# Attention scores from two rounded 32-bit parts, two heads at once on the two halves of TensorE's rows

## The chip, the core and the metric

One core of a Trainium2 chip runs the whole program. The metric is the device time of one execution in microseconds (us), the median of several runs. A core has five engines that are programmed apart and meet by semaphores: TensorE (PE; its weight loads have rows of their own, PEld), VectorE (DVE), ScalarE (ACT), GpSimd (POOL) and SyncE (SP), which only issues transfers here. A queue name with a q (SPq, ACTq) stands for the transfers that the engine issues.

## What is computed

A "macaron" block on 16 sequences of 512 tokens and 256 features: half a feed-forward step with 16 routed and 2 shared experts, then attention with 16 heads of 16 features, then half a feed-forward step again. Cut to what matters:

```python
def attn(x, Wq, bq, Wk, bk, Wv, bv, Wf, bf):          # x: (16, 512, 256), already layer-normed
    q, k, v = heads(x @ Wq + bq), heads(x @ Wk + bk), heads(x @ Wv + bv)
    # heads 0..7 look back only, heads 8..15 look ahead only, with a slope on the distance
    fwd = slopes * tril(rel) + triu(-1e9, 1)
    bwd = slopes * triu(-rel) + tril(-1e9, -1)
    scores = einsum('bhqd,bhkd->bhqk', q, k) / sqrt(16) + concatenate([fwd, bwd])
    out = einsum('bhqk,bhkd->bhqd', softmax(scores), v)
    return out.transpose(0, 2, 1, 3).reshape(B, S, D) @ Wf + bf

x = x + 0.5 * ffn(layernorm(x))
x = x + attn(layernorm(x))
x = x + 0.5 * ffn(layernorm(x))
```

## The kernel before

**Stages.** The feed-forward step works in groups of sequences: layer norm, routing, the two shared experts, then the routed tokens are scattered to memory sorted by expert, read back as tiles of 256 rows ("tile transpose" L1071, "tile hidden" L1081, "tile out" L1092), written and gathered again. Attention runs sequence by sequence (b = 0 to 15) in four groups of four heads (g = 0 to 3). Feed-forward tiles of both layers are woven in between, so that all engines serve both.

**One group of heads.** Scores are computed twice. First with queries on the rows ("row", L1132), only to get each query's largest score: ten units u of up to 512 columns for the four heads, each in one bank of PSUM. A unit of the first four is one product of 512 columns; one of the next four is a product of 384 and one of 128 columns; the last two have two of 256. A further product adds -1e9 beyond the diagonal: the identity times a mask of -1e9 (L1148). DVE takes the maxima (L1566, L1559). Their negatives are split into two parts (L1657, L1660), turned by a small transposition on PE (L1154), copied by ACT (L1346) and sent by a transfer into two further rows of the query stack (L1349). Then the scores are computed with keys on the rows ("score", L1165), now with the maximum already subtracted by those two rows, again in ten units. ACT takes the exponential of each (L1325), POOL zeroes what lies beyond the diagonal (L1782), and PE multiplies by the values (L1185, four heads side by side on 32 columns of the array each).

**The stacks.** `q_stack` and `k_stack` hold, for each head, the numbers that one product contracts: six blocks of 16 rows that pair three bfloat16 parts of q with three of k (QB, KB), three rows for the slope, and two for the maximum: 99 or 101 rows. ACT (L1302), DVE (L1643), ACT (L1307) and POOL (L1769) split q and k into the three parts, and SP scatters them in 6 transfers for q and 6 for k for each half m of the heads (L922). The stacks exist once: the half m = 0 (groups 0 and 1) of the next sequence can be scattered only after the last score of group 1, the half m = 1 after that of group 3. PE waits for the last of the 12 transfers before the first "row" of the half.

**What sets the order.** `schedule()` plays the program through with a list of due times and costs and writes one order for each engine; it also hands out PSUM's eight banks (`BANKS`: at most three at a time for "row", two for "score", one for the outputs, three for the feed-forward work). Each engine then runs its list strictly in order.

**Shape of PE's work.** A product whose contraction has at most 64 rows and starts at row 0 or 64 uses one half of the array's rows: "tile out" does so for its two halves (L1092). A product with 32 output columns uses a quarter of the columns (L1185, L1154). All others use the whole array. Below, a change from one of these three shapes to another in PE's order is called a change of shape.

## Time and profile before

| | |
|---|---|
| median of 3 runs | 2115.41 us (2111.2 to 2123.95) |
| the profiled execution, its own time | 2112.85 us, of which the span is 2111.1 us |
| PE busy | 1678.2 us (79% of the span) |
| DVE busy | 1477.3 us (70%) |
| ACT busy | 1041.3 us (49%) |
| POOL busy | 946.5 us (45%) |
| first "row" to last "score" | 384 to 1901 us |

How to read it: a busy time is the union of an engine's instructions. A matmul's duration holds the time in which its results drain, which overlaps the next matmul. What a matmul costs is therefore read from the step between two starts. Attention fills 384 to 1901 us; the stretch before is the first feed-forward group, the one behind is the last.

### The profile page before, as it was taken

Reading aid. Unit: us, or ns where it says so; the run is one execution under the profiler, and the core shown is the slowest. Engines: PE = TensorE matmul, PEld = TensorE weight load, DVE = VectorE, ACT = ScalarE, POOL = GpSimd, SP = SyncE. Lnnn points to the kernel's source line nnn. Section 1 sums busy time; section 2 is a strip of 40 time slices with the busy share of each in tenths; the row PEclk is TensorE's granted clock in tenths of the full one; section 3 lists DMA queues with packets and bytes.
Section 4 is the critical chain, followed back from the end, with each engine's and each line's share of the span. In section 5 each row is a group of like instructions: output and inputs, shape, how many; then the busy total and the mean of one; then the engine's idle time right before and its main releaser. Section 6 shows DMA issues by size and latency. Waiting matters only on the chain. (4 is left out here: it accounts for less than half of the span.)

```text
span 2111.1 us, 35275 instructions
## 1 busy us (share of the span) xinstructions
PE 1678.2 (79%) x10696; PEld 1106.3 (52%) x10696; DVE 1477.3 (70%) x3920; ACT 1041.3 (49%) x2263; POOL 946.5 (45%) x999
## 2 busy tenths in 40 slices
PE   2769885778898898889887988889887777897571
PEld 2656664546565564555454655656554444565440
DVE  4886666779866675787968778677786875765352
ACT  3335543355555655555544565556554344554241
POOL 1653337554524231546534444253545656131544
PEclk8889996899999998998988999999998779899786
DMA  7368862747878777565648776586647686865995
GB/s 211 137 217 291 257 201 93 143 97 202 231 181 237 190 222 168 157 102 123 134 100 232 191 182 184 147 202 143 172 96 145 208 236 169 207 205 177 322 362 171
DMA packets 327978, 392.79 MB, mean 186 GB/s; under 512 B 40296, under 2 KB 269032, under 8 KB 327784
## 3 DMA queue, kind: packets, MB, share of 16 engines
q1 hardware_dynamic: 260816, 267.81, 49.1%
q0 software_dynamic: 24576, 67.14, 11.1%
q10 hardware_dynamic: 42400, 55.59, 8.4%
q8 instruction: 88, 1.44, 0.3%
q14 instruction: 98, 0.80, 0.1%
HBM read 188.58 MB, written 155.19 MB: 163 GB/s over the span
## 5 line engine op out<-in xcount | busy, mean ns | idle before, releaser
L1325 ACT ACTIVATE p_buf<-bank 128x512 f32<-128x512 f32 x640 | 358.4, 598 | 228.1 <-PE bank L1165 193.0
L1566 DVE TENSOR_REDUCE row_max<-bank 128x1 f32<-128x512 f32 (+2 forms) x768 | 348.4, 502 | 119.8 <-PE bank L1148 117.6
L1782 POOL TENSOR_SCALAR_AFFINE_SELECT p_buf<-p_buf 128x512 f32<-128x512 f32 x256 | 160.4, 641 | 387.2 <-ACT p_buf L1325 386.2
L1132 PE MATMUL bank<-k_stack,q_stack 99*128 99x512 bf16 (+3 forms) x1024 | 249.9, 319 | 37.0 <-issue 29.8
L1165 PE MATMUL bank<-q_stack,k_stack 101*128 101x512 bf16 (+3 forms) x1024 | 239.3, 318 | 50.1 <-DMA q_stack<-shift_t 37.1
L1725 POOL DMA_INDIRECT sorted_x<-xn,position x224 | 221.2, 988 | 91.7 <-issue 52.1
L1748 POOL DMA_INDIRECT y_tok<-sorted_y,position x192 | 185.4, 966 | 130.2 <-DVE x_att L1637 52.1
L1185 PE MATMUL bank<-p_buf,v_rows 128*32 128x512 f32 (+3 forms) x2048 | 188.1, 468 | 37.5 <-POOL p_buf L1782 36.7
L1291 ACT ACTIVATE t_y<-bank 128x256 f32<-128x256 f32 x406 | 133.3, 381 | 128.3 <-PE bank L1092 106.3
L1081 PE MATMUL bank<-t_xt,t_w 128*128 128x256 f32 x548 | 157.0, 413 | 34.8 <-DMA t_w<-expert_w 25.8
L1619 DVE SCALAR_TENSOR_TENSOR t_g<-t_th,bank 64x256 f32<-64x256 f32 x203 | 82.5, 407 | 136.3 <-ACT t_th L1282 134.6
L1148 PE MATMUL bank<-cbf 128*128 128x256 bf16 (+1 forms) x640 | 169.4, 265 | 0.0
L1165 PEld LDWEIGHTS bank<-q_stack,k_stack 101*128 101x128 bf16 x1024 | 85.0, 101 | 153.3 <-issue 52.2
L1132 PEld LDWEIGHTS bank<-k_stack,q_stack 99*128 99x128 bf16 x1024 | 95.0, 103 | 130.9 <-issue 70.6
L1276 ACT ACTIVATE t_xt<-bank 128x512 f32<-128x512 f32 x203 | 118.9, 595 | 71.3 <-PE bank L1071 62.7
L1282 ACT ACTIVATE t_th<-bank 64x256 f32<-64x256 f32 x203 | 76.2, 375 | 131.1 <-PE bank L1081 106.8
L1081 PEld LDWEIGHTS bank<-t_xt,t_w 128*128 128x128 f32 x548 | 101.7, 202 | 67.4 <-DMA t_w<-expert_w 31.3
L1755 POOL TENSOR_TENSOR hs_buf<-h_buf,hs_buf 128x512 fp32r<-128x512 f32 x64 | 81.8, 1278 | 119.9 <-ACT hs_buf L1246 119.2
L1667 DVE RECIPROCAL den<-den 128x128 f32<-128x128 f32 x128 | 109.2, 910 | 30.5 <-DMA den<-o_store 30.3
L1624 DVE TENSOR_TENSOR t_h<-bank,t_g 64x128 f32<-64x128 f32 x406 | 119.2, 294 | 13.3
L974 PE MATMUL bank<-w_down,hs_buf 128*128 128x256 f32 x256 | 82.5, 322 | 52.1 <-POOL hs_buf L1755 50.4
L1092 PE MATMUL bank<-t_w,t_h 64*128 64x256 f32 x548 | 100.5, 444 | 17.0 <-DVE t_h L1624 15.6
(193 smaller groups left out, 3807.6 us busy)
## 6 DMA issues: line engine op xcount, KB each, us to landing
t_w<-expert_w SPq DMA_DIRECT2D x137, 256.0 KB
t_x<-sorted_x SPq DMA_DIRECT2D x137, 256.0 KB, 4.2
sorted_y<-t_y SPq DMA_DIRECT2D x137, 256.0 KB
q_stack<-qk_part SPq DMA_DIRECT2D x192, 128.0 KB
k_stack<-qk_part SPq DMA_DIRECT2D x192, 128.0 KB, 6.8
sorted_x<-zeros SPq DMA_DIRECT2D x69, 256.0 KB, 3.6
p_buf<-expert_w SPq DMA_DIRECT2D x66, 256.0 KB, 4.8
p_buf<-sorted_x SPq DMA_DIRECT2D x66, 256.0 KB, 4.7
```

Of the source, the lines that this page charges most:

```text
L1081: ins = pe.matmul(ps[:, 0:RT], weights[:, P * d:P * d + P], xt[:, d, :], start=(d == 0), stop=(d == ND - 1))
L1132: pe.matmul(ps[:, col:col + k1 - k0], q_stack[0:ROWS_S, h, P * qt:P * qt + P], k_stack[0:ROWS_S, h, k0:k1], start=(n == 0), stop=False, sk ...
L1148: ins = pe.matmul(dst, ident_bf, mask, start=False, stop=True, skip_group_check=True)
L1165: ins = pe.matmul(ps[:, col:col + q1 - q0], k_stack[0:ROWS_P, h, P * kt:P * kt + P], q_stack[0:ROWS_P, h, q0:q1], start=(n == 0), stop=Tru ...
L1185: ins = pe.matmul(ps[VR * hh:VR * hh + VR, q0:q1], v_rows[b % 2][:, v0:v0 + VR], p_of(u)[:, col:col + q1 - q0], start=(r == 0), stop=(r == 2),
L1291: act.activation(t_y[i][:, t, :], psum("ty", *of, t)[:, 0:D], ACT.Copy).then_inc(*ty_out.step(*of, t))
L1325: act.activation(p_of(u), psum("score", *of)[:, :], ACT.Exp).then_inc(*exp_done.step(*of))
L1566: ins = dve.tensor_reduce(row_max[g % 2][:, n:n + 1], src[:, col:col + q1 - q0], X, ALU.max)
L1624: dve.tensor_tensor(t_h[i][ME * t:ME * t + ME, :], ps[ME:P, at], t_g[:, at], ALU.mult).then_inc(*th_step.step(*of, "u", t))
L1725: pool.indirect_dma_start(sorted_x[l, group_of(l, b)], bass.IndirectOffsetOnAxis(ap=position[:, b, k, t:t + 1], axis=0), xn[buffer][:, t, ...
L1748: pool.indirect_dma_start(y[:, k, t, :], None, sorted_y[l, g], bass.IndirectOffsetOnAxis(ap=position[:, b, k, t:t + 1], axis=0)).then_inc( ...
L1782: pool.affine_select(blocks, blocks, [[0, GH], [1 if ahead else -1, P]], ALU.is_ge, zero, base=0, channel_multiplier=-1 if ahead else 1).t ...
```

## The change

The split is now into two parts that keep 32-bit storage (fp32r, the rounded form that the matmul reads), so three blocks of 16 rows pair them, with two rows for the slope and two for the maximum: 50 or 52 rows. Two heads share a stack slot, one on rows 0 to 51, one on rows 64 to 115. A pair of units of two such heads (`rows`, `scores`) is issued in turn, one on each half of the array, into two banks, and signalled once. The mask product contracts 64 rows in place of 128, one on each half; its two factors give sums of terms up to -2^30 beyond the diagonal. The third part's steps on ACT and POOL are gone. The scatter still has 6 transfers for q and 6 for k of 128 KB each, now 64 rows of 2 KB; the maxima go in two transfers instead of one, one for each half. `BANKS` allows four banks for "row" and four for "score".

```diff
-ROWS_S = 6 * HD + 3
+QB = (0, 0, 1)
+KB = (0, 1, 0)
+ROWS_Q = len(QB) * HD
+ROWS_S = ROWS_Q + 2
 ROWS_P = ROWS_S + 2
-QB = (0, 0, 0, 1, 1, 2)
-KB = (0, 1, 2, 0, 1, 0)
...
-BANKS = {"row": 3, "score": 2, "out": 1, "fill": 3, "wide": 6}
+BANKS = {"row": 4, "score": 4, "out": 1, "fill": 3, "wide": 6}
...
-                part(at + 0.38 * u, "PE", 0.33 if u < 4 else 0.4, piece, *stacks, takes=takes, lag=0.3)
+                part(at + 0.76 * v, "PE", 0.45 if v < 2 else 0.5, rows, *stacks, takes=takes, lag=0.3)
...
-                part(t + at + 0.6 + 0.1 * w, "ACT", 0.62, rest, (qk, "DVE"))
-                part(t + at + 0.6 + 0.1 * w, "POOL", 1.17, rest, (rest, "ACT"))
...
-        q_stack = sb("q_stack", [P, H, S], BF16)
-        k_stack = sb("k_stack", [P, H, S], BF16)
+        q_stack = sb("q_stack", [P, SLOTS, S], F32R)
+        k_stack = sb("k_stack", [P, SLOTS, S], F32R)
...
-                    sp.wait_ge(*qk_third.at(*of))
+                    sp.wait_ge(*qk_step.at(*of))
                     stack, parts = ((q_stack, QB), (k_stack, KB))[n]
-                    for blk in range(6):
-                        sp.dma_start(stack[HD * blk:HD * blk + HD, HB * m:HB * m + HB, :],
-                                     qk_part[n][:, parts[blk], :]).then_inc(*scattered[n, m].step(b, blk))
+                    for blk in range(3):
+                        for half in range(2):
+                            low = HALF * half
+                            sp.dma_start(stack[low + HD * blk:low + HD * blk + HD, SLOTS // 2 * m:SLOTS // 2 * (m + 1), :]
+                                         .bitcast(F32), qk_part[n][low:low + HALF, parts[blk], :].bitcast(F32)
+                                         ).then_inc(*scattered[n, m].step(b, blk, half))
...
+                    both_u = 2 * v, 2 * v + 1
+                    two = [take(("row", b, g, u), max_done, b, g, u) for u in both_u]
+                    for n in range(len(unit_tiles(g, 2 * v))):
+                        for ps, u in zip(two, both_u):
+                            hh, r = unit_tiles(g, u)[n]
+                            (low, slot), qt, col = place_of(g, hh), row_tile(g, hh, r), row_col(g, hh, r)
+                            k0, k1 = keys(GH * g + hh, qt)
+                            at = slice(low, low + ROWS_S)
+                            pe.matmul(ps[:, col:col + k1 - k0], q_stack[at, slot, P * qt:P * qt + P],
+                                      k_stack[at, slot, k0:k1], start=(n == 0), stop=False, skip_group_check=True)
...
+                    for ps, low in zip(two, (0, HALF)):
+                        at = slice(low, low + HALF)
+                        mask = right[at, :]
...
+                        ins = pe.matmul(dst, left[at, :], mask, start=False, stop=True, skip_group_check=True)
...
-                    act.dma_start(q_stack[ROWS_S:ROWS_P, GH * p:GH * p + GH, :], shift_t[p % 2][:, :]
-                                  ).then_inc(*shift_row[p % 2].step(b, p))
+                    for half in range(2):
+                        low = HALF * half
+                        act.dma_start(q_stack[low + ROWS_S:low + ROWS_P, 2 * p:2 * p + 2, :].bitcast(F32),
+                                      shift_t[p % 2][GH * NT * half:GH * NT * half + GH * NT, :]
+                                      ).then_inc(*shift_row[p % 2].step(b, p, half))
```

PE's order, at the first "row" units of sequence 8, group 1. In the kernel before, L1165 is a score, L1132 a row product and L1148 its mask; the bank written stands ahead of the arrow.

```order
L1165 MATMUL bank2<-q_stack,k_stack 128x384
L1165 MATMUL bank2<-q_stack,k_stack 128x128
L1132 MATMUL bank5<-k_stack,q_stack 128x512
L1148 MATMUL bank5<-cbf 128x128
L1165 MATMUL bank7<-q_stack,k_stack 128x384
L1165 MATMUL bank7<-q_stack,k_stack 128x128
L1132 MATMUL bank6<-k_stack,q_stack 128x512
L1148 MATMUL bank6<-cbf 128x128
L1165 MATMUL bank0<-q_stack,k_stack 128x384
L1165 MATMUL bank0<-q_stack,k_stack 128x128
L1185 MATMUL bank4<-p_buf0,v_rows1 32x512 x4
```

The same place in the changed kernel, where L1197 is a score, L1160 a row product, L1176 its mask and L1217 the values.

```order
L1197 MATMUL bank7<-q_stack,k_stack 128x384
L1197 MATMUL bank1<-q_stack,k_stack 128x384
L1197 MATMUL bank7<-q_stack,k_stack 128x128
L1197 MATMUL bank1<-q_stack,k_stack 128x128
L1160 MATMUL bank6<-k_stack,q_stack 128x512
L1160 MATMUL bank2<-k_stack,q_stack 128x512
L1176 MATMUL bank6<-cbf 128x128
L1176 MATMUL bank2<-cbf 128x128
L1217 MATMUL bank5<-p_buf0,v_rows1 32x512 x4
```

Each product now stands beside its twin in another bank, and the two kinds of score work are next to each other in the half-array shape. Counted over PE's whole order, the changes of shape are 804 before and 1096 in the changed kernel. Before, a step into the whole-array shape begins with a bfloat16 product (mostly L1132, L1165) 224 times and with a 32-bit one 152 times; a step into the half-array shape begins with a 32-bit one 201 times; 227 steps go into the quarter-column shape. In the changed kernel these are 8, 398, 470 and 220.

ACT's order around the maxima's transfer of one group, in the kernel before: L1325 is an exponential, L1346 and L1349 the copy and the transfer of the maxima, L1332 and L1335 the output.

```order
L1325 ACTIVATE p_buf1<-bank2 128x512
L1325 ACTIVATE p_buf1<-bank7 128x512
L1325 ACTIVATE p_buf1<-bank0 128x512
L1325 ACTIVATE p_buf1<-bank3 128x512
L1346 ACTIVATE shift_t0<-bank2 32x128
L1349 DMA q_stack<-shift_t0 2x16x128
L1325 ACTIVATE p_buf2<-bank1 128x512
L1325 ACTIVATE p_buf2<-bank0 128x512
L1332 ACTIVATE o_raw<-bank4 128x512
L1335 DMA o_store<-o_raw 128x512
```

The same group in the changed kernel (L1353 is an exponential, L1374 and L1379 the maxima's copy and transfers, L1360 and L1363 the output).

```order
L1353 ACTIVATE p_buf1<-bank2 128x512
L1353 ACTIVATE p_buf1<-bank4 128x512
L1353 ACTIVATE p_buf1<-bank7 128x512
L1353 ACTIVATE p_buf1<-bank1 128x512
L1353 ACTIVATE p_buf2<-bank4 128x512
L1353 ACTIVATE p_buf2<-bank3 128x512
L1374 ACTIVATE shift_t0<-bank1 32x128
L1379 DMA q_stack<-shift_t0 2x8x128 x2
L1360 ACTIVATE o_raw<-bank5 128x512
L1363 DMA o_store<-o_raw 128x512
```

Here the maxima's copy stands two exponentials later against the group that is being finished, and it issues two transfers.

## Rows read from the trace of the kernel before

**Rows 1.** The page: busy us of each engine, share of the span, instructions.
```profile
PE 1678.2 (79%) x10696; PEld 1106.3 (52%) x10696; DVE 1477.3 (70%) x3920; ACT 1041.3 (49%) x2263; POOL 946.5 (45%) x999
```
**Rows 2.** Windows: length; busy us (count) PE, PEld, DVE, ACT, POOL; clock; DMA; GB/s.
```profile
384.00:1901.00 1517.00, 1290.65 (x8624) 815.47 (x8625) 1135.65 (x2843) 812.76 (x1731) 675.92 (x731) 0.93 0.69 173
1541.00:1555.00 14.00, 10.07 (x75) 6.69 (x75) 10.28 (x31) 7.58 (x17) 1.28 (x3) 1.00 0.89 137
1700.00:1800.00 100.00, 80.30 (x493) 49.56 (x493) 65.23 (x160) 46.88 (x99) 55.51 (x59) 0.86 0.75 205
```
**Rows 3.** Waits from 384 to 1901 us: who for whom, total us, times, longest.
```profile
PE bank L1165 <- DMA q_stack<-shift_t: 37.1, 15, 6.2
PE bank L1185 <- POOL p_buf L1782: 36.7, 40, 4.2
DVE row_max L1566 <- PE bank L1148: 117.6, 65, 9.9
ACT p_buf L1325 <- PE bank L1165: 193.0, 127, 13.0
SPq L922 <- PE bank L1165: 122.5, 23, 18.8
```
**Rows 4.** Timeline of PE: start us, us, line, operation, count; bfloat16 units.
```profile
1227.17 0.38 PE L1132 MATMUL bank<-k_stack,q_stack 99*128 99x512 bf16 x1
1227.39 0.22 PE L1148 MATMUL bank<-cbf 128*128 128x128 bf16 x1
1227.44 0.38 PE L1132 MATMUL bank<-k_stack,q_stack 99*128 99x512 bf16 x1
...
1231.26 0.39 PE L1132 MATMUL bank<-k_stack,q_stack 99*128 99x384 bf16 x2
...
1231.60 0.38 PE L1132 MATMUL bank<-k_stack,q_stack 99*128 99x384 bf16 x2
```
**Rows 5.** Timeline of PE: rounded 32-bit products of 512 and 256 columns.
```profile
1211.44 0.40 PE L975 MATMUL bank<-act_t,w_attn 128*128 128x512 f32 x1
1211.68 0.40 PE L976 MATMUL bank<-act_t,w_attn 128*128 128x512 f32 x1
1212.00 0.70 PE L1092 MATMUL bank<-t_w,t_h 64*128 64x256 f32 x4
1212.64 0.39 PE L1132 MATMUL bank<-k_stack,q_stack 99*128 99x512 bf16 x1
...
1203.41 0.28 PE L975 MATMUL bank<-w_down,hs_buf 128*128 128x256 f32 x1
1203.52 0.28 PE L976 MATMUL bank<-w_down,hs_buf 128*128 128x256 f32 x1
```
**Rows 6.** Timeline of PE: full 32-bit products, and a small one of another shape.
```profile
1216.11 1.03 PE L1081 MATMUL bank<-t_xt,t_w 128*128 128x256 f32 x4
1216.97 0.60 PE L1165 MATMUL bank<-q_stack,k_stack 101*128 101x512 bf16 x3
...
1244.75 0.23 PE L1154 MATMUL bank<-cbf,shift 128*32 128x128 bf16 x1
1244.91 0.39 PE L1165 MATMUL bank<-q_stack,k_stack 101*128 101x384 bf16 x2
```
**Rows 7.** Page, costliest groups: weight loads of bfloat16 and of 32 bits, mean ns.
```profile
L1165 PEld LDWEIGHTS bank<-q_stack,k_stack 101*128 101x128 bf16 x1024 | 85.0, 101 | 153.3 <-issue 52.2
L1081 PEld LDWEIGHTS bank<-t_xt,t_w 128*128 128x128 f32 x548 | 101.7, 202 | 67.4 <-DMA t_w<-expert_w 31.3
```
**Rows 8.** One line each: count, ns min/median/max, first and last start.
```profile
L1307 ACT ACTIVATE qk_part<-rest x64: 616/630/652, 365.6 to 1798.5; 128x512 bf16<-128x512 f32 x64
L1769 POOL TENSOR_TENSOR qk_part<-rest,qk_part x64: 1146/1162/1413, 366.3 to 1799.2; 128x512 bf16<-128x512 f32 x64
L1349 ACTq DMA_DIRECT2D q_stack<-shift_t x64: 623/683/1274, 396.1 to 1889.7; - x64
```
**Rows 9.** Timeline of SP, the six transfers of q for one half.
```profile
1540.65 4.39 SPq L922 DMA_DIRECT2D q_stack<-qk_part  x6
```

More of the change, by code:

```diff
@@ L40 @@
 RT = 256
-N_BIAS = 6
+N_BIAS = 10
 N_ONES = 3
@@ L393, in gathering @@
         tail = y_buffer(l, b) > 0
-        needs = [(("score", B - 1, NG - 1, UNITS - 1), "PE")] if tail else []
+        needs = [(("scores", B - 1, NG - 1, PAIRS - 1), "PE")] if tail else []
         if (l, b) == (0, 0):
@@ L464, in schedule @@
             stacks = [(("qk put", b, g // 2, w), "SP") for w in range(2)]
[L465 to L468 removed]
+            for v in range(PAIRS):
+                rows, two = ("rows", b, g, v), [("row", b, g, u) for u in (2 * v, 2 * v + 1)]
+                takes = [bank("row", piece, (piece, "DVE")) for piece in two]
+                if v == 0:
                     takes.append(("pair", ("pair", b, g), [(("shift out", b, g), "ACT landed")]))
[L470 to L471 removed]
+                part(at + 0.76 * v, "PE", 0.45 if v < 2 else 0.5, rows, *stacks, takes=takes, lag=0.3)
+                for piece in two:
+                    part(at + 0.76 * v, "DVE", 0.83 if v in (2, 3) else 0.69, piece, (rows, "PE"))
             shift, out = ("shift", b, g), ("shift out", b, g)
@@ L476, in schedule @@
             part(at + 3.9, "ACT", 1.1, out, (out, "PE"), lag=3.4)
-            for u in range(UNITS):
-                score, c = ("score", b, g, u), set_of(u)
-                s = at + 4.9 + 0.38 * u
-                part(s, "PE", 0.3, score, (out, "ACT"), takes=[bank("score", score, (score, "ACT"))], lag=0.3)
-                takes = [(f"p{c}", ("p", b, g, c), [(("values", b, g, c), "PE")])] if u == SETS[c][0] else []
-                part(s, "ACT", 0.6, score, (score, "PE"), takes=takes)
+            for v in range(PAIRS):
+                scores, two = ("scores", b, g, v), [("score", b, g, u) for u in (2 * v, 2 * v + 1)]
+                s = at + 4.9 + 0.76 * v
+                part(s, "PE", 0.4, scores, (out, "ACT"),
+                     takes=[bank("score", score, (score, "ACT")) for score in two], lag=0.3)
+                for score in two:
+                    u, c = score[3], set_of(score[3])
+                    takes = [(f"p{c}", ("p", b, g, c), [(("values", b, g, c), "PE")])] if u == SETS[c][0] else []
+                    part(s, "ACT", 0.6, score, (scores, "PE"), takes=takes)
             for c, (u0, u1) in enumerate(SETS):
@@ L515, in schedule @@
                 part(t + at + 0.3 * w, "DVE", 0.75, qk, (qk, "ACT"))
-                part(t + at + 0.6 + 0.1 * w, "ACT", 0.62, rest, (qk, "DVE"))
-                part(t + at + 0.6 + 0.1 * w, "POOL", 1.17, rest, (rest, "ACT"))
-                used = [(("score", b - 1, 2 * m + 1, UNITS - 1), "PE")] if b else [(("stack rows",), "SP")]
-                part(t + (12.7, 20.7)[m], "SP", 3.6, put, (rest, "POOL"), *used, lag=6.0)
+                used = [(("scores", b - 1, 2 * m + 1, PAIRS - 1), "PE")] if b else [(("stack rows",), "SP")]
+                part(t + (12.7, 20.7)[m], "SP", 3.6, put, (qk, "DVE"), *used, lag=6.0)
         for half in range(2):
```

246 lines of the change are left out of this document (120 added, 126 removed).

## The prediction

> **What bounds the kernel now.** I read the page first: PE is the busiest engine with 1678 us, DVE has 1477, ACT 1041 [rows 1]. Then the windows: attention runs from 384 to 1901 us, and there PE is busy for 1291 of 1517 us (85%), DVE for 1136 (75%), ACT for 813, at a mean granted clock of 0.93 [rows 2]. Then the waits of that stretch: ACT waits for a score product 193 us in all, DVE for a masked row product 118 us, while PE waits for ACT or DVE seldom; its longest totals are the transfer of the maxima, 37 us, and POOL's mask, 37 us [rows 3]. So the evacuating engines wait for PE more than PE for them, and no engine is full: PE's order is the nearest thing to a bound, with latencies in its gaps. A second loop runs beside it. SP waits 122 us for the last score before it may scatter the next half [rows 3], then the first six transfers alone take 4.4 us to issue [rows 9], and the transfer engines are 0.89 busy in such a stretch with PE still working [rows 2]. Two halves alternate, so most of that is covered.
>
> **PE's products.** A unit of the row product steps by 1227.44 - 1227.17 = 0.27 us with a 128-column mask and by 1231.60 - 1231.26 = 0.34 us with a 256-column one [rows 4]. 0.22 of either is the 512 columns, which is also a score unit. One group: 4 x 0.27 + 6 x 0.34 + 10 x 0.22 = 5.3 us, and 64 groups 340 us.
>
> After, 512 columns of fp32r step by 0.24 us and 256 by 0.115 [rows 5]. Do two half-array products overlap? L1092 is such a pair, in full 32 bits: four records, and the next instruction starts 0.64 us later [rows 5]. Two products of the same width one after the other on the whole array, L1081, take 0.86 us [rows 6]. Half of 0.86 is 0.43, so the pair overlaps fully and 0.21 us is something else (below). Per pair of units I take the price of one: 512 columns and mask 0.24 + 0.05; 384 and 128 with a 256-column mask 0.18 + 0.06 + 0.11; twice 256 with its mask 0.23 + 0.11. Rows of one group: 2 x 0.29 + 2 x 0.35 + 0.34 = 1.6 us. Scores: 2 x 0.24 + 2 x (0.18 + 0.11) + 0.23 = 1.3 us, where the 128-column piece is given the 0.11 us of a weight load that nothing longer covers. 64 x 2.9 = 186 us. **Saved: 340 - 186 = 154 us.**
>
> No fp32r product of 128 columns is in the trace, and each group has 4 pairs of them. Bounds: 0.06 us (by column) and 0.215 us (the rate of full 32 bits, half of L1092's 0.43). At the upper end 4 x about 0.13 us x 64 = 32 us of the saving are gone. I take the lower, since 256 and 512 columns of this type step by column; both ends go into the range.
>
> **PE's changes of shape.** The small transposition L1154 has 128 columns, 0.05 us by column, and the next product starts 0.16 us later [rows 6]: the change itself costs 0.10 us. After L1092 and L976 the two changes and one uncovered 32-bit weight load come to (0.32 - 0.24) + 0.21 = 0.3 us [rows 5]. So a change into a bfloat16 product, or to 32 output columns, costs 0.10 to 0.11 us, and one into a 32-bit product with 128 output columns 0.20, since its load comes on top. That fits the loads' records, 101 ns for bfloat16 and 202 for 32 bits [rows 7]. By the counts under the change: before 224 x 0.10 + 353 x 0.20 + 227 x 0.11 = 118 us, after 8 x 0.10 + 868 x 0.20 + 220 x 0.11 = 199 us. **Lost: 81 us**, half the saving. PE's net relief is 154 - 81 = 73 us (41 with slow 128-column pieces).
>
> The Trainium skill, "TensorEngine Tiling (Array Packing)", Key Properties, says that changing the tiling mode drains TensorE; by that rule the trace agrees, at 0.10 us each. Its page "TensorE: Matmul & The Clock Gate", Weight-path perf modes, has the fast weight load only for types other than fp32; the two load durations agree. By rule and by row alike the relief is 73 us, where a count of products alone gives 154.
>
> **From PE to the end.** All of this lies between 384 and 1901 us. At clock 0.93 the 73 us are 78 us of time. PE is busy 85% there, and the transfer, maxima and mask latencies stay; DVE would stand near 79%. I let three quarters pass: 0.75 x 78 = 58 us.
>
> **The rest.** ACT loses 64 x 0.63 us of the third part and gains a second maxima transfer to issue, 64 x 0.68 us [rows 8]: +3 us, nothing. But the second transfer starts 0.68 us after the first, PE waits for both, and in ACT's order the exponentials of the next group stand behind it. PE's 15 waits for that transfer [rows 3] grow by 15 x 0.7 = 10 us. POOL loses 64 x 1.16 = 74 us [rows 8]; POOL is busy 45%, its values' masks make PE wait 37 us over 40 times, and I credit 4 us. The chain that is removed (ACT, POOL) ended before the scatter, which waits for the scores instead, so its length earns nothing; where that cover is gone it would be 1.8 us once for each half. The scatter has the same 12 transfers and the same bytes: zero. More instructions that split the attention weights, under 2 us. Sum: -58 + 10 - 4 = -52 us.
>
> The profiled execution has 2112.85 us of its own; that gives 2061. The median of the runs lies 2.6 us above it, so **2064 us**.
>
> **The rivals.**
> - *More passes than PE's relief* (0.18). The four banks for scores let PE run two pairs ahead; ACT's 193 us and DVE's 118 us of waits shrink, and both halves' loops with them. If all 78 us pass and a sixth of the 311 us of waits besides, the time is 2115 - 78 - 52 + 6 = 1991. Against it: eight banks now carry claims of 12, and the feed-forward work shares them.
> - *Slow 128-column pieces* (0.17). Relief 41 us, 44 at the clock, 33 passing, + 6: 2115 - 27 = 2088.
> - *Evacuation sets the pace* (0.13). DVE's maxima and ACT's exponentials are unchanged in number and size, and the scatter's loop is not shorter. If these bound the stretch, PE's relief becomes idle time: 2115 + 6 = 2121, at most 1% from before. For it: DVE 75% busy and in order. Against: DVE waits 118 us for PE. The Trainium skill, "TensorEngine Tiling (Array Packing)", PSUM Bottleneck, warns that tiling speeds TensorE and not the evacuation; no row here shows that it binds.
> - *The clock gives it back* (0.14), the other side. A stretch in which PE is busy 80% has a granted clock of 0.86 where the whole has 0.93 [rows 2]. PE's 1291 us minus 78 in the same 1517 would be 80%. If the clock goes to 0.86 by that, what is left, 1213 us, becomes 1213 x 0.93 / 0.86 = 1312 us, 99 more than without, against 78 saved: 21 slower, and with the 10 us of the maxima and banks that starve the feed-forward tiles, 2115 + 31 = 2146. It decides from a clock of 0.93 x 1213 / 1291 = 0.87 down. Against it: the two levels, 1.2 and 2.4 GHz, mix in every stretch, and 0.86 also came with feed-forward work that waited for transfers.
> - *The change does not do what it says*: the twins do not overlap with this type and width. Then rows and scores cost 2 x 186 = 372 us against 340, plus 81: over 100 us slower, 2230. The pair L1092 speaks against it (0.03, counted as slower).
>
> **How the numbers follow.** The forecast itself (-52, 2064, own range 2035 to 2092) has 0.35. Each way by about 1%, 21 us, is what a measurement of this kernel can tell from no change. Faster by over 1%, below 2094: forecast 0.34, more passes 0.18, most of the slow pieces 0.12, sum 0.64. Slower, above 2137: the clock 0.13 and no overlap 0.03, 0.16. Within: 0.20. The range 2000 to 2130 leaves out half of "more passes" (0.06 to 0.09) and nearly all of the slower ones.
>
> **What would show it.** In the changed profile: L1160 and L1197 in pairs with steps of 0.24 us a pair (right) or 0.48 (no overlap); the 384 and 128-column pair with its mask 0.35 us (0.50 if slow); PE's busy time in attention down by some 70 us while its instructions are fewer; granted clock still 0.92 or more; DVE near 79% there; the wait of L1197 for the maxima's transfer up by some 10 us. The prediction is wrong if the granted clock falls below 0.88, if a change of shape costs more than 0.10 us between 32-bit products, or if PE starts to wait for row_max and p_buf (the evacuation).

## The result, and the profile after

The changed kernel takes 2090.8 us (median; 2088.1 to 2095.6) against 2119.5 us of the kernel before on the same chip: a ratio of 0.987, 95% interval 0.983 to 0.991. That is 1.3% faster, some 27 us, where 52 us (2064) were forecast. It lies inside the range, and on the right side, but half of the size is missing. The profiled execution has a span of 2086.3 us (before 2111.1). Ratios here and below are taken over executions in the kernel's faster state alone, on the same chip, and can differ a little from the quotient of two medians.

The page of the changed kernel, busy us of each engine, share of the span and instructions:
```profile
PE 1646.8 (79%) x10696; PEld 1114.7 (53%) x10696; DVE 1467.1 (70%) x3924; ACT 999.8 (48%) x2205; POOL 874.8 (42%) x935
```
Against [rows 1], PE lost 31 us of busy time, POOL 72, ACT 42, DVE 10. The windows (length; busy us and count of PE, PEld, DVE, ACT, POOL; granted clock; DMA share; GB/s) of the parts ahead of, in and behind attention:
```profile
0.00:386.00 386.00, 271.00 (x1494) 214.20 (x1494) 251.20 (x814) 158.62 (x364) 181.41 (x179) 0.88 0.65 200
386.00:1874.00 1488.00, 1257.11 (x8612) 821.66 (x8612) 1123.33 (x2845) 771.13 (x1664) 608.08 (x670) 0.89 0.69 176
1874.00:2086.00 212.00, 118.69 (x593) 78.85 (x592) 92.61 (x266) 70.01 (x178) 85.34 (x87) 0.79 0.78 261
```
Attention took 1517 us before [rows 2] and takes 1488 now; the parts around it (384 and 210 us, now 386 and 212) did not move. The granted clock fell from 0.93 to 0.89. The waits from 386 to 1874 us (who for whom, total us, times, longest), to be laid beside [rows 3]:
```profile
PE bank L1197 <- DMA q_stack<-shift_t: 54.0, 23, 7.4
PE bank L1217 <- POOL p_buf L1802: 18.8, 22, 2.2
PE bank L1160 <- DVE row_max L1595: 13.9, 20, 1.8
DVE row_max L1595 <- PE bank L1176: 87.5, 63, 6.5
ACT p_buf L1353 <- PE bank L1197: 149.1, 101, 7.0
```
ACT waits for scores 149 us instead of 193, DVE for masked rows 88 instead of 118, PE for POOL's mask 19 instead of 37, and PE for the transfer of the maxima 54 instead of 37.

The timeline of PE (start us, length us, line, operation, shape, merged count) at full clock, four places:
```profile
453.24 0.73 PE L1197 MATMUL bank<-q_stack,k_stack 52*128 52x512 f32 x4
453.91 0.66 PE L1023 MATMUL bank<-c,xn 128*128 128x128 f32 x4
...
1203.43 0.50 PE L1160 MATMUL bank<-k_stack,q_stack 50*128 50x384 f32 x4
1203.77 0.28 PE L1176 MATMUL bank<-cbf 64*128 64x256 bf16 x2
1203.81 0.48 PE L1197 MATMUL bank<-q_stack,k_stack 52*128 52x512 f32 x2
1204.13 0.40 PE L1160 MATMUL bank<-k_stack,q_stack 50*128 50x384 f32 x4
1204.37 0.28 PE L1176 MATMUL bank<-cbf 64*128 64x256 bf16 x2
...
1220.12 0.51 PE L1160 MATMUL bank<-k_stack,q_stack 50*128 50x384 f32 x4
1220.46 0.29 PE L1176 MATMUL bank<-cbf 64*128 64x256 bf16 x2
1220.50 0.48 PE L1160 MATMUL bank<-k_stack,q_stack 50*128 50x384 f32 x4
...
1284.84 0.50 PE L1197 MATMUL bank<-q_stack,k_stack 52*128 52x256 f32 x4
1285.18 0.39 PE L1160 MATMUL bank<-k_stack,q_stack 50*128 50x512 f32 x2
```
Four records (384 and 128 columns on either half) step by 1203.77 - 1203.43 = 0.34 us with their first load uncovered and by 0.24 us with it covered (1204.13 to 1204.37). Two score products of 512 columns step by 0.32 us behind a mask. A whole pair of units with its mask takes 0.38 us (1220.12 to 1220.50), where two units took 2 x 0.34 in [rows 4]. Two pairs of 512 columns and the change behind them take 453.91 - 453.24 = 0.67 us, and two 256-column products on either half take 1285.18 - 1284.84 = 0.34 us. The two halves do run side by side; the twins' records start 3 ns apart. These places are typical. Over the whole trace, at full clock, where PE did not wait and the next product is a half-array one too, a pair of score units takes 0.34 us whatever its columns (medians 0.337, 0.340 and 0.342 us of 36, 12 and 22 pairs), and a pair of row units with its mask 0.384 us (medians 0.384, 0.384 and 0.387 us of 21, 47 and 22). The 0.236 us that the columns of a 512 pair would allow stands at 3 of the 36.

### The profile page after: what moved, and what is told of

The parts are those of the page before. It is cut to its first block and busy times, and to the rows that moved or that the text cites. A ratio compares the mean times of both kernels' runs of the same rounds, so it can differ in the third digit from the quotient of the medians.

```text
span 2086.3 us, 35743 instructions
## 1 busy us (share of the span) xinstructions
PE 1646.8 (79%) x10696; PEld 1114.7 (53%) x10696; DVE 1467.1 (70%) x3924; ACT 999.8 (48%) x2205; POOL 874.8 (42%) x935
## 5 line engine op out<-in xcount | busy, mean ns | idle before, releaser
L1353 ACT ACTIVATE p_buf<-bank 128x512 f32<-128x512 f32 x640 | 345.8, 601 | 199.3 <-PE bank L1197 149.1
L1197 PE MATMUL bank<-q_stack,k_stack 52*128 52x512 f32 (+3 forms) x1024 | 172.8, 408 | 78.0 <-DMA q_stack<-shift_t 54.0
L1217 PE MATMUL bank<-p_buf,v_rows 128*32 128x512 f32 (+3 forms) x2048 | 202.9, 499 | 20.5 <-POOL p_buf L1802 18.8
L1160 PE MATMUL bank<-k_stack,q_stack 50*128 50x512 f32 (+3 forms) x1024 | 171.0, 399 | 57.5 <-issue 20.9
L1106 PE MATMUL bank<-t_xt,t_w 128*128 128x256 f32 x548 | 164.7, 429 | 19.2 <-DMA t_w<-expert_w 12.8
L1197 PEld LDWEIGHTS bank<-q_stack,k_stack 52*128 52x128 f32 x1024 | 95.5, 214 | 155.8 <-DMA q_stack<-shift_t 62.8
L1160 PEld LDWEIGHTS bank<-k_stack,q_stack 50*128 50x128 f32 x1024 | 96.7, 207 | 120.9 <-issue 83.9
L1742 POOL TENSOR_TENSOR rstd_ffn<-var_eps_ffn,minus_half 128x4 f32<-128x4 f32 x32 | 33.6, 1050 | 181.0 <-DVE var_eps_ffn L1446 165.4
```

Source lines behind the costliest of these rows:

```text
L1106: ins = pe.matmul(ps[:, 0:RT], weights[:, P * d:P * d + P], xt[:, d, :], start=(d == 0), stop=(d == ND - 1))
L1160: pe.matmul(ps[:, col:col + k1 - k0], q_stack[at, slot, P * qt:P * qt + P], k_stack[at, slot, k0:k1], start=(n == 0), stop=False, skip_gro ...
L1197: ins = pe.matmul(ps[:, col:col + q1 - q0], k_stack[at, slot, P * kt:P * kt + P], q_stack[at, slot, q0:q1], start=(n == 0), stop=True, ski ...
L1217: ins = pe.matmul(ps[VR * hh:VR * hh + VR, q0:q1], v_rows[b % 2][:, v0:v0 + VR], p_of(u)[:, col:col + q1 - q0], start=(r == 0), stop=(r == 2),
L1353: act.activation(p_of(u), psum("score", *of)[:, :], ACT.Exp).then_inc(*exp_done.step(*of))
```

## Experiments: is PE's relief worth its time?

My theory after the result: the speed of PE's products is not what sets the pace, and what PE is relieved of turns into idle time and lower clock. The rival is the forecast's step, three quarters of the relief pass to the end. Where a ratio is given in this and the next sections, it is to the kernel before on the same chip; 1% is 21 us. The first four of these kernels keep the planner's order of the kernel that they start from, since nothing that the planner reads is touched (the traces of the first and of the kernel before agree in all 10056 products that both have); the fifth doesn't.

The recorded expectations use letters of their own. In this section theory A is that half-array products keep the granted clock low, theory B that a relief of PE which other latencies fill up lowers the clock, and theory E, in the run with four banks, the theory above.

**The kernel before without its mask products** (L1148 is left out, and L1132 ends the unit):
```diff
-                    ins = pe.matmul(dst, ident_bf, mask, start=False, stop=True, skip_group_check=True)
```


> The kernel before without its mask products (so the maxima are taken over masked columns too); nothing else is moved. A pure relief of PE: 4 x 0.05 + 6 x 0.11 = 0.88 us a group, 56 us in all, with no half-array product and no change of shape added. Theory A (half-array products keep the granted clock low): the clock in attention stays at 0.92 to 0.93 and the time falls by 40 to 50 us, ratio to before 0.976 to 0.981. Theory B (any relief of PE that other latencies fill up lowers the clock): clock 0.89 to 0.91, time down by 15 to 30 us, ratio 0.986 to 0.993.

Measured: 2104.6 us, ratio 0.998 (0.995 to 1.002). PE has 56 us less to do at full clock, and at most 0.5%, 11 us, of it arrives. Neither A nor B forecast that: B had the clock right (0.90) and the time not. Its window of attention and its two waits for PE, from 384 to 1901 us:
```profile
384.00:1901.00 1517.00, 1264.06 (x7985) 775.32 (x7986) 1138.62 (x2843) 809.93 (x1732) 677.23 (x731) 0.90 0.69 173
```
```profile
ACT p_buf L1312 <- PE bank L1152: 187.8, 131, 13.7
DVE row_max L1553 <- PE bank L1132: 112.7, 60, 10.7
```
The stretch is as long as before, 1517 us (this profiled execution, at 2115 us, is one of the longer ones of its kernel; the ratio above is the measure of the time). ACT and DVE wait for PE as long as in [rows 3] (188 and 113 us against 193 and 118). So those waits are not a measure of PE's pace. That a product comes late because of its place in PE's order, and of what that order waited for, fits this but is not shown by it. The clock's own record has 295 us of the stretch at 1.2 GHz instead of 220: (295 - 220) / 2 = 37 of the 56 us went there, the other 19 into idle time.

**The same omission with four banks each for rows and scores**, one more order:
```diff
-BANKS = {"row": 3, "score": 2, "out": 1, "fill": 3, "wide": 6}
+BANKS = {"row": 4, "score": 4, "out": 1, "fill": 3, "wide": 6}
```


> The kernel before with four banks for rows and scores and without the mask products of the rows (the masked part of the scores' maxima is left out: some 56 us of PE's time at full clock). With the bank limits of before the same omission gave 0.998. Theory E (PE's time is not the bound, and what it is relieved of becomes idle time and a lower granted clock): as with the banks alone, 0.990 (0.986 to 0.993), granted clock in attention about 0.90. Rival I (PE's relief does pay once products may run further ahead, which is why the whole change brought more than the sum of its parts): 0.990 minus half of 56 us, 0.975 to 0.98.

Measured: 2095.1 us, 0.989 (0.985 to 0.994), beside 0.990 (0.987 to 0.994) with the banks alone (below): 0.1% for 56 us again, and by the two intervals 0.7%, 14 us, at the most. Windows of attention, with the masks (first) and without:
```profile
382.00:1883.00 1501.00, 1291.63 (x8612) 816.36 (x8611) 1134.77 (x2840) 807.60 (x1727) 678.63 (x732) 0.93 0.69 174
```
```profile
381.00:1878.00 1497.00, 1255.21 (x7968) 762.95 (x7967) 1131.29 (x2840) 804.83 (x1726) 676.52 (x732) 0.92 0.69 174
```
Here the time at 1.2 GHz grew only from 212 to 243 us: 15 us went to the clock, some 3 to the end, and the remaining 38 us are idle time. In the other order the clock took 37. The gain is missing either way, so a lower clock isn't needed to explain that it is missing. By the Trainium skill, "TensorE: Matmul & The Clock Gate", Part 1, the gate follows how busy PE has been; the traces agree in direction within each pair of runs (busy 85.1%, 83.3% and a clock of 0.93, 0.90; 86.1%, 83.8% and 0.93, 0.92), but not across kernels: the changed one, busy 84.5%, has 0.89.

**The changed kernel with each pair of mask products issued twice**, same order:
```diff
-                    for ps, low in zip(two, (0, HALF)):
+                    for ps, low in zip(two * 2, (0, HALF) * 2):
```


> The changed kernel with each pair of mask products issued twice: 0.44 us a group, 28 us more of PE's time in all, with no change of shape more. Theory B (what is added to PE while others set the pace is paid by the clock, which rises): within 6 us of the changed kernel, with the granted clock in attention up from 0.887 to about 0.90. If PE's time passes on: 20 to 30 us above the changed kernel and the same clock.

Measured: 2099.3 us, 0.990 (0.986 to 0.994), against 0.987: some 28 us more for PE cost 0.3%, 6 us. The two intervals allow up to 0.8%, 17 us, so this run alone does not rule out that half of a load arrives. The clock did not rise to 0.90, as theory B expected, but stayed at 0.89.

**The changed kernel with each pair as one product over the whole array**, same order, with 782 changes of shape instead of 1096:
```diff
-                            pe.matmul(ps[:, col:col + k1 - k0], q_stack[at, slot, P * qt:P * qt + P],
-                                      k_stack[at, slot, k0:k1], start=(n == 0), stop=False, skip_group_check=True)
...
+                        at = slice(0, HALF + ROWS_S)
+                        pe.matmul(ps[:, col:col + k1 - k0], q_stack[at, slot, P * qt:P * qt + P],
+                                  k_stack[at, slot, k0:k1], start=(n == 0), stop=False, skip_group_check=True)
```


> The changed kernel with each pair of products replaced by one product over the whole array (it contracts both heads' rows together, so the scores are a mixture, and the second bank of a pair is read as it stands; exponentials are of scaled scores; 10 small transfers more at the start). The same columns and weight loads on PE, but no half-array score work: changes of shape 1096 to 783, 62 us less by the priced changes. Theory A: the granted clock in attention returns to 0.92 or more, and the time is 60 to 100 us below the changed kernel (1990 to 2030). Theory B: the clock stays at 0.88 or falls further with the extra relief, and the time is 15 to 35 us below the changed kernel (2055 to 2075).

Measured: 2076.4 us, 0.982 (0.975 to 0.988). Attention from 392 to 1864 us:
```profile
392.00:1864.00 1472.00, 1214.41 (x7267) 810.48 (x7267) 1120.29 (x2844) 767.48 (x1663) 607.34 (x669) 0.89 0.69 177
```
PE's work at full clock is some 40 us less: 314 changes fewer at 0.10 us are 31, the busy time by the clock falls by 1257.11 x 0.89 - 1214.41 x 0.89 = 38. (The 62 us of the expectation priced a change at the forecast's 0.20.) The ratio falls by 0.6%, 12 us: three tenths, in intervals that overlap and allow up to some 28 us. This is the largest share that any of the runs shows. The clock stayed at 0.89 with no half-array product left in the score work, so theory A is out.

**The changed kernel with a planner that prefers a product of the shape just used** (851 changes instead of 1096, hence another order):
```diff
+                    rank = (part[0] - (SAME_SHAPE if n == "PE" and shape_of(kind) == last_shape else 0), part[1])
-                    if best is not None and best[0][:2] < part[:2]:
+                    if best is not None and best[3] < rank:
```


> The changed kernel with a planner that lets a part of PE's work go first by up to 4 of its units when it has the shape of the part before it. Only the orders change: changes of shape 1096 to 852, 45 us less of PE's time by the priced changes. If the changes of shape are what ate the gain and PE's time passes on: 25 to 45 us below the changed kernel (2045 to 2065). If the clock gives the relief back (theory B): 5 to 20 us below. A worse order for the other engines could make it slower than the changed kernel.

Measured: 2098.5 us, 0.991 (0.988 to 0.994): 245 changes fewer, and not faster than the changed kernel. The clock in attention is 0.875, with 379 us at 1.2 GHz. Its order is another one, so by what the section on orders below finds, this run can't tell the two theories apart.

The forecast's step asked for 2% from the first run (42 us) and got 0.2%, 0.5% at the most; the second says the same in another order. These two settle it for the kernel before. In the changed kernel the doubled masks and the whole-array products point the same way, with intervals that leave room for a larger share.

## Experiments: the smaller terms

**The changed kernel with one transfer of the maxima from the second sequence on:**
```diff
-                        pe.wait_ge(*shift_row[g % 2].at(b, g, 1))
+                        pe.wait_ge(*shift_row[g % 2].at(b, g, int(b == 0)))
...
-                    for half in range(2):
+                    for half in range(2 if b == 0 else 1):
```


> The changed kernel without the second transfer of the maxima from the second sequence on (heads on the upper half of the rows keep old maxima). If the second transfer matters as forecast (0.68 us later for the waits of PE and on ACT): 10 to 20 us below the changed kernel, and PE's wait for this transfer in attention falls from 54 us to below 40. If it does not: within 5 us of it.

Measured: 2089.0 us, 0.988 (0.982 to 0.994). Its wait for that transfer, from 390 to 1880 us:
```profile
PE bank L1197 <- DMA q_stack<-shift_t: 30.3, 15, 5.5
```
The wait fell from 54 to 30 us, and the time did not move. The second transfer does make PE wait some 20 us, and no cost in time shows. The intervals are 0.4 and 0.6% wide on either side, so the 10 us of the forecast are not ruled out by this run.

**The kernel before without the third part's steps on ACT and POOL** (lines of both engines taken out, the stack's third block filled from the second part):
```diff
-QB = (0, 0, 0, 1, 1, 2)
-KB = (0, 1, 2, 0, 1, 0)
+QB = (0, 0, 0, 1, 1, 1)
+KB = (0, 1, 1, 0, 1, 0)
```


> The kernel before without the third part of q and k: its steps on ACT (64 x 0.63 us) and POOL (64 x 1.16 us) are gone, DVE writes the second part where the rest went, and the blocks that paired the third part hold the second. PE's products are those of before. Theory C (the gain comes from what is taken off ACT, POOL and the chain to the scatter): 15 to 30 us below before, ratio 0.986 to 0.993. Theory D (the gain is the pairs on PE and their banks): within 5 us of before.

Measured: 2125.0 us, 1.004 (1.001 to 1.007). In attention ACT is busy for 783 us instead of 813 and POOL for 608 instead of 676, and the kernel is a little slower. Neither theory of the expectation has that (C asked for 0.986 to 0.993, D for 5 us at most). The planner's input changed, so its order did too; that was the first sign of what the section on orders finds.

## Experiments: the bank limits

The theory of this section: the 1.3% come from the limits of PSUM banks, which let PE run two pairs ahead of ACT and DVE. The first two expectations call it theory E, the later ones, in the next section too, theory B; C and D are those of the run without the third part. First both limits moved in the kernel before (the BANKS line above), and the score limit taken back in the changed kernel (`"score": 2`):

> The kernel before with the limits of the changed kernel on PSUM's banks: four for row units, four for score units, in place of three and two. Only the orders and the banks change. Theory E (the banks bring the gain, since ACT and DVE wait less for PE): 15 to 30 us below before. Theories C and D: within 8 us of it.

> The changed kernel with two banks for scores in place of four, so one pair can be out at a time. Theory E: 15 to 40 us above the changed kernel, that is back at before or over it, and ACT's wait for scores up from 149 us. Theory C: within 8 us of the changed kernel.

Measured: 2092.6 us, 0.990 (0.987 to 0.994), and 2112.4 us, 0.998 (0.996 to 1.001). Both came out as this theory expected, and alone they looked like proof: the limits give the gain to the old kernel and their lack takes it from the new. ACT's wait for scores in the one (384 to 1895 us) and the other (384 to 1901 us):
```profile
ACT p_buf L1325 <- PE bank L1165: 124.7, 87, 8.4
```
```profile
ACT p_buf L1353 <- PE bank L1197: 210.9, 135, 6.3
```
Then each limit alone in the kernel before (`"row": 4` with two for scores, and `"score": 4` with three for rows), and six each in the changed kernel:

> The kernel before with one of its two bank limits moved: four banks for the row products instead of three, scores stay at two. Both limits at four gave 0.990. Theory S (the limit of scores carries the gain, since ACT's waits for scores, 193 us in all, fell to 125 with both limits moved): this run stays at 1.00 (0.997 to 1.003) and ACT's wait for scores stays near 190 us. Rival R (the limit of rows carries it, since DVE's wait for row products fell from 118 to 85 us): 0.990 here.

> The kernel before with the other limit moved: four banks for scores instead of two, rows stay at three. Theory S: 0.990 as with both, ACT's wait for scores near 125 us. Rival R: 1.00. If both limits are needed, both runs lie between, near 0.995.

> The changed kernel with limits of six banks for rows and for scores (all eight are shared with the other products). Theory B (room for products ahead of ACT and DVE is what brought the gain): a little more of it, 0.980 to 0.984 against 0.987 for the changed kernel, ACT's wait for scores under 149 us. Rival (four are enough, beyond that the eight banks are the limit and the feed-forward products starve): 0.987 to 0.995, with longer waits for L1106's and L1117's products.

Measured: 1.004 (1.002 to 1.006), 1.006 (1.004 to 1.009) and 0.987 (0.983 to 0.990). Each limit alone is slower than neither, though both widen what PE may do and though ACT's wait for scores fell in both (to 164 and 147 us); both together are faster. Neither theory S nor R had that, and the six banks did not bring the 0.980 to 0.984 that the theory of banks asked for. It is what one sees if the numbers are not the limits' but the orders': the planner takes a piece when a bank is free, so any limit reorders attention from its first products on.

## Experiments: what an order alone is worth

Theory N: any change of the planner's tables shuffles PE's order, and that moves the time by up to 1%. Two nudges that touch nothing of the work: 2.2 us instead of 2.15 for DVE's moments, and 0.62 instead of 0.6 for one exponential, on the kernel before, the changed one, and the one before with four banks each.
```diff
-        part(at, "DVE", 2.15, moments, ready, takes=[("mom_" + kind, ("mom", kind, l, b), [(norm, "ACT")])])
+        part(at, "DVE", 2.2, moments, ready, takes=[("mom_" + kind, ("mom", kind, l, b), [(norm, "ACT")])])
```
```diff
-                part(s, "ACT", 0.6, score, (score, "PE"), takes=takes)
+                part(s, "ACT", 0.62, score, (score, "PE"), takes=takes)
```
What the second nudge does to PE's order in the kernel before, at its first place (a row that stands there only before with -, only in the nudged kernel with +; w_attn are projections of a next sequence):
```order
 L1165 MATMUL bank<-q_stack,k_stack 128x128
+L1165 MATMUL bank<-q_stack,k_stack 128x256 x2
 L974 MATMUL bank<-act_t,w_attn 128x512
 L975 MATMUL bank<-act_t,w_attn 128x512
 L976 MATMUL bank<-act_t,w_attn 128x512
 L974 MATMUL bank<-act_t,w_attn 128x512
 L975 MATMUL bank<-act_t,w_attn 128x512
 L976 MATMUL bank<-act_t,w_attn 128x512
-L1165 MATMUL bank<-q_stack,k_stack 128x256 x2
```
One of the last score units moves ahead of two projections there, and some 230 such places follow (some 330 under the first nudge).

> The kernel before, with one cost in the planner's table changed that has nothing to do with the scores: 2.2 us instead of 2.15 for DVE's moments. The work is the same, its order on PE is not (the planner's choices part from the first products on and shift all through attention). Theory N (what any change of the tables does to the order is worth up to 1% either way, so the 0.990 of both bank limits, the 1.004 and 1.006 of each alone and the 0.998 of the changed kernel with two score banks are mostly order): away from 1.000 by more than its interval, by 0.3 to 1%. Theory B (the order is neutral, the limits are what counts): 1.000 within 0.3%.

> The kernel before with another such nudge: the planner's cost of one exponential on ACT 0.62 us instead of 0.6. Theory N: 0.3 to 1% from 1.000, either way, and another value than the first nudge gives. Theory B: 1.000 within 0.3%.

> The changed kernel with the first nudge (moments 2.2 us). Theory N: its ratio to the kernel before scatters like that of the other orders, 0.980 to 0.995 against 0.987; if the mean of the three orders of the changed kernel against that of the three of before is below 0.992, the whole change is worth more than the order. Theory B: 0.987 within 0.3%.

> The changed kernel with the second nudge (exponential 0.62 us). Theory N: between 0.980 and 0.995 and away from the first nudge's value; theory B: 0.987 within 0.3%.

> The kernel before with four banks for rows and four for scores, and the first nudge of the planner's costs (moments 2.2 us), which gave 1.007 on the kernel before. Theory N (order alone gives a spread of about 1%; the 0.990 of the two limits was a lucky order): anywhere from 0.990 to 1.010, near 1.00, three orders with a mean like that of the kernel before, 1.005. Theory B (both limits together do bring 1 to 1.5%, the order comes on top): 0.985 to 0.997.

> The same with the second nudge (exponential 0.62 us), which gave 1.009 on the kernel before. Theory N: near 1.00, 0.990 to 1.010. Theory B: 0.985 to 0.998, and the mean of the three orders with four banks each at most 0.995, beside 1.005 of the three orders of the kernel before.

Measured, ratio to the kernel before with its interval:

| kernel | as it is | first nudge | second nudge | mean |
|---|---|---|---|---|
| before | 1.000 | 1.007 (1.002 to 1.012) | 1.009 (1.003 to 1.015) | 1.005 |
| before, four banks each | 0.990 (0.987 to 0.994) | 1.006 (1.003 to 1.008) | 0.994 (0.991 to 0.996) | 0.997 |
| changed | 0.987 (0.983 to 0.991) | 0.997 (0.991 to 1.003) | 1.007 (1.002 to 1.013) | 0.997 |

Theory N holds in its main point, and the spread is larger than it said for the changed kernel (0.980 to 0.995 was expected): a cost in a table that is off by 0.02 us took that kernel from 0.987 to 1.007. Theory B fails in five of the six runs; only the last one, 0.994, lies in its range too, and the mean that it asked for, 0.995 at the most, did not come. Within a row the ratios spread by a standard deviation of 0.8% (the three rows pooled). The mean of three orders is then known to 0.8 / sqrt(3) = 0.46%, and the difference of two means to 0.65%; with six degrees of freedom its 95% interval is 2.45 x 0.65 = 1.6% either way. So the change without the luck of one order is worth -0.8%, somewhere between -2.4% and +0.8%, and the limits alone would do as well. Nine orders do not tell these from nothing, nor from each other. The line that was drawn beforehand, the changed row's mean below 0.992 of the first row's, is met by a hair (0.992), which decides nothing.

The spread holds some error of the measurement too. The four nudged ratios of the first and third rows share seven executions of the kernel before, with a median of 2105.4 us where the other chips of these experiments gave 2112.2 to 2115.9. If those seven were low by chance, the four ratios are some 0.4% too high together, and the spread is 0.7% instead of 0.8%. The difference between the first and the third row does not hang on that; the second row's nudges were measured on another chip.

The profile of the changed kernel under the second nudge, attention and two waits from 387 to 1897 us:
```profile
387.00:1897.00 1510.00, 1250.92 (x8614) 822.08 (x8614) 1119.63 (x2845) 772.90 (x1664) 607.70 (x669) 0.89 0.67 173
```
```profile
ACT p_buf L1353 <- PE bank L1197: 202.5, 107, 9.3
DVE row_max L1595 <- PE bank L1176: 68.2, 52, 5.8
```
The work of every engine and the clock are those of the changed kernel (PE 1251 us against 1257, 0.89), and the stretch is 22 us longer. ACT's wait for scores is back at 203 us, as long as in the kernel before, with the limits and the pairs still there: so the fall of that wait, 193 to 149 us, can't be credited to the change. It doesn't follow the time either: in the kernel before under the first nudge, slower by 0.7%, it stood at 160 us (384 to 1890 us):
```profile
ACT p_buf L1325 <- PE bank L1165: 160.4, 108, 13.4
```

## Why the prediction came out as it did

**PE's products and changes of shape: the net relief right, both of its terms wrong.** The forecast had 0.24 us for a pair of 512 columns, 0.24 for the columns of 384 and 128 (0.29 with a load), 0.35 with the latter's mask, in all 2.9 us a group. The medians above are 0.34 us for any pair of score units and 0.384 us for any pair of row units with its mask: 5 x 0.34 + 5 x 0.384 = 3.6 us a group, 232 us for all, so the saving is 340 - 232 = 108 us and not 154. What was priced at nothing for most pairs is a part of the next 32-bit weight load, about 0.1 us between one unit and the next (0.337 against the 0.236 of a covered load). The forecast put that load into the changes of shape, at 0.20 us for each change into a 32-bit product. But a change itself costs 0.094 us behind a score (0.43 against 0.34 us), and 0.12 to 0.17 us behind a mask pair, above the 0.10 us that the prediction named as a sign of being wrong. (1096 - 804) x 0.094 = 27 us, and by an estimate some 9 us more for those behind masks, make 36 us lost, not 81.

The two errors, 46 and 45 us, cancel: 108 - 36 = 72 us of net relief against 73 forecast. That is luck, and not a confirmation of the prices. From the window rows, busy time by clock, 1290.65 x 0.93 - 1257.11 x 0.89 = 81.

The twins overlap in full: in the run with one whole-array product for each pair, the same units step by 0.320 us (512 columns, 52 of them) and 0.385 us (rows with mask, 35 of 512 columns). So "the change does not do what it says" is out, and so is "slow 128-column pieces", since the pairs that hold such pieces take no longer than the others. That a change drains PE, which the Trainium skill states in "TensorEngine Tiling (Array Packing)", Key Properties, shows at 0.094 us here.

**From PE to the end: the step that failed.** "I let three quarters pass: 0.75 x 78 = 58 us" rested on PE's 85% and on the waits of ACT and DVE for PE. The runs show 0.06 of 56 us (at most 0.2), again nearly nothing in a second order (at most 0.25), 0.2 of a load of 28 us (at most 0.6), and 0.3 of the 40 us of the whole-array products (at most 0.7). By 0.06 to 0.3 the term is -4 to -22 us instead of -58. The reading behind it was wrong in a way that [rows 3] did not show. The likely reason, which no run isolates, is that ACT waits for a score because the score stands behind something else in PE's order, or is itself late by a transfer or a maximum; a faster product doesn't move its place. The forecast for DVE followed from the same step: 79% busy was expected, 1123 / 1488 = 75% came. PE's own idle time in attention is as long as before, 1488 - 1257 = 231 us against 226, in a stretch that is 29 us shorter.

**The clock.** PE's capacity in attention, its length less half the time at 1.2 GHz, was 1517 - 110 = 1407 us and is 1488 - 168 = 1320. Of the 87 us, 58 are clock and 29 time, while the work fell by 72 to 81. So in the changed kernel itself the clock took most of the relief, and the rival "the clock gives it back" had its arithmetic half right (0.89 came, not 0.86). Two things speak against it as the cause of the missing gain: without the masks and with four banks the clock stayed at 0.92 and the gain was missing all the same, and with whole-array products the clock stayed where it was and most of the relief was missing too. No run holds the changed work at 0.93, so what its lower clock costs is not separated; nor is it known why all changed kernels stand at 0.89 or below, since theory A of the half-array products is out. The nearest rival by mechanism is "evacuation sets the pace" in its consequence, PE's relief becomes idle time, 2121; in its cause it is not shown, since DVE is at 75% and waits.

**The second transfer of the maxima:** forecast +10 us of wait and of time. The wait grew by 17 us; the time it costs, by the run with one transfer, is 0 by the middle values (0.988 against 0.987), with 10 us inside the intervals. Right in the trace, and in the sum probably wrong by the same error as above: a wait of PE's was priced as time.

**POOL, ACT, the third part's chain, the scatter:** forecast -4 us, the rest 0. PE's waits for POOL's mask fell by 18 us; the run without the third part, at 1.004 in an order of its own, shows no gain. Against the order's spread, 4 us can't be seen.

**What was missing altogether:** the order as a term of its own. The change rewrites the planner's parts, costs and limits, so the new kernel has another of many orders, and orders of the same work spread by a standard deviation of 0.8%, 17 us. With the failed step mended the sum would have been about -10 to -25 us, some 2100, with that spread around it. The measured -27 us lie within one deviation of that. The sign came true, and how much of that is the order's luck can't be told: the ratio of the same change under the second nudge is 1.007 to the kernel before, and within 0.2% of before under that nudge (1.009).

**Still open** is what does set the pace of attention. No engine is full, the speed of PE's products isn't it by the runs in the kernel before, and ACT, POOL and the transfer of the maxima gave nothing that shows when relieved (ACT and POOL in another order). What these runs leave is the order itself, with the latencies between engines that each order strings together differently; no run isolates one of them. None of the kernels tried that leave nothing out beats the changed one: its own limits raised to six give 0.987 too.

## What to carry to other kernels

Before a relief is passed on to the end, ask the kernel for its exchange rate: take some work off the busiest engine with the order held, and see what arrives; here 56 us off an engine that was 85% busy gave 3 us, 11 at the most. Check each term of a forecast against the trace even where the total comes true; here two errors of some 45 us cancelled. Where a planner or a scheduler makes the order, time the same work in two or three neutral orders first; a gain below their spread (here 0.8%) belongs to the order as long as several orders of both versions don't say otherwise, however narrow the interval of one comparison is. Waits of other engines for the busy one do not say what its speed is worth: here they stayed at 188 and 113 us with that work gone.

## What the runs showed of the hardware that I had not expected

A relieved PE wasn't granted the same clock: with 56 us less work in the same 1517 us, the time at 1.2 GHz rose from 220 to 295 us (clock 0.927 to 0.903). And the changed kernels all stand at 0.875 to 0.89 in attention, with PE 82 to 85% busy, where the old ones, masks included, have 0.92 to 0.94 with 85 to 86%, and the old one without masks and with four banks has 0.92 with 84%. So the busy share alone does not give the clock. Busy time from the page hides a part of what a change saves: PE's fell by 34 us in attention, its work at full clock by 72 to 81.

Two half-array products of rounded 32-bit type start 3 ns apart and take the time of one. What a pair of units takes does not follow its columns here, 0.34 us for 512 columns, for 384 with 128 and for twice 256, with some 0.1 us of a weight load in it for the first that nothing covers. Their weight loads are not shorter for having half of the rows: 214 ns with 52 rows against 202 with all 128 of L1081 [rows 7]:
```profile
L1197 PEld LDWEIGHTS bank<-q_stack,k_stack 52*128 52x128 f32 x1024 | 95.5, 214 | 155.8 <-DMA q_stack<-shift_t 62.8 <-issue 44.9 <-ACT p_buf L1353 23.5
```
